# Cross-attention: the transpose of a pair's maxima on VectorE in place of TensorE, and the place of the last two softmax sums

## The reference

```python
x = x + self_attention(layernorm(x), Wq, Wk, Wv, Wo)     # causal, 8 groups of 4 heads of 16
x = x + cross_attention(layernorm(x), ctx, ctx)
x = x + feed_forward(layernorm(x), w_gate, w_up, w_down)

def cross_attention(q, k, v):
    b, d, m = q.shape                      # 4, 512, 512
    qh = q.reshape(b * 8, 64, m); kh = k.reshape(b * 8, 64, -1); vh = v.reshape(b * 8, 64, -1)
    qk = einsum('bdm,bdn->bmn', qh, kh) / sqrt(64)
    sm = softmax(qk, axis=-1)
    return einsum('bmn,bcn->bcm', sm, vh).reshape(b, 512, m)
```

## Time and profile before

| | us |
|---|---|
| Kernel, median of 3 runs (799.4 to 804.82) | 802.62 |
| Profiled execution, its own time | 804.03 |
| Its span, first to last instruction | 801.9 |
| TensorE matmul busy | 769.0 (96%) |
| VectorE busy | 639.2 (80%) |
| ScalarE busy | 491.6 (61%) |
| GpSimd busy | 423.4 (53%) |

### The profile page before, as it was taken

How to read it: one execution, slowest core, us unless ns; L and a number is a source line. 1 busy time by engine, 2 the same in 40 slices (tenths; PEclk the granted TensorE clock), 3 DMA queues, 4 the chain that set the end, 5 groups by cost and what they waited for, 6 DMA issues and landing times.

```text
span 801.9 us, 15448 instructions
## 1 busy us (share of the span) xinstructions
PE 769.0 (96%) x4902; PEld 423.2 (53%) x4902; DVE 639.2 (80%) x1905; ACT 491.6 (61%) x844; POOL 423.4 (53%) x458
## 2 busy tenths in 40 slices
PE   7999999999999999998998999999998899999997
PEld 6777544444444444444875555555543455555543
DVE  7676888889888888971689678888876798888883
ACT  4665467667767767765465455555556565576564
POOL 5554479999999600000334367777785344423321
PEclk9999999999999999999999899999999999999999
DMA  8898665445445212201485534444420011000001
GB/s 290 303 380 290 197 163 138 130 128 142 131 118 148 70 52 64 63 3 53 154 289 193 170 96 130 126 125 120 119 72 11 13 41 40 18 24 27 27 19 47
DMA packets 65760, 94.79 MB, mean 118 GB/s; under 512 B 26928, under 2 KB 38448, under 8 KB 64144
## 3 DMA queue, kind: packets, MB, share of 16 engines
q1 hardware_dynamic: 61216, 80.77, 31.8%
q0 software_dynamic: 3952, 12.98, 6.0%
q10 hardware_dynamic: 512, 0.07, 0.1%
HBM read 72.88 MB, written 20.51 MB: 116 GB/s over the span
## 4 chain that ended last, share of the span: by engine, by line
PE 32%; DVE 11%; issue 4%; ACT 2%; POOL 1%; DMA 1%; SPq 1%; ACTq 0%; DVEq 0%; POOLq 0%
PE r_p L1697 12%; PE r_p L1631 4%; PE r_pn L1644 4%; PE r_p L1727 3%; PE r_pn L1727 3%; DVE r_mx L1408 3%; DVE r_kl L1420 3%; PE r_p L1597 2%; PE r_p L1711 2%; DVE r_stats L1378 1%; DVE r_total L1438 1%; DVE tok L1397 1%; DVE r_inv L1445 1%; PE r_p L1579 1%; DVE r_xl L1391 1%
## 5 line engine op out<-in xcount | busy, mean ns | idle before, releaser
L787 ACT ACTIVATE b_probs<-ab_j 128x512 f32<-128x512 f32 (+1 forms) x352 | 177.1, 560 | 26.7 <-PE ab_j L852 15.8
L148 DVE CUSTOM_DVE_ANT_0 b_junk<-ab_t,mask_qk 128x128 bf16<-128x128 f32 (+2 forms) x243 | 108.8, 486 | 26.9 <-PE ab_t L128 26.8
L852 PE MATMUL ab_j<-qs,ks 98*128 98x512 bf16 (+1 forms) x352 | 123.3, 365 | 1.6 <-DVE a_rest L533 0.8
L1276 ACT ACTIVATE r_probs<-r_p 128x512 f32<-128x512 f32 x128 | 69.5, 599 | 72.3 <-PE r_p L1631 71.0
L148 DVE CUSTOM_DVE_ANT_0 b_junk<-ab_e,mask_qk 128x256 bf16<-128x256 f32 (+2 forms) x237 | 103.7, 482 | 1.8 <-PE ab_e L128 1.5
L1408 DVE TENSOR_REDUCE r_mx<-r_p 128x1 f32<-128x512 f32 x128 | 82.4, 675 | 23.9 <-PE r_p L1597 22.0
L1174 POOL TENSOR_TENSOR r_halves<-r_probs 128x1024 f32<-128x1024 f32 x32 | 77.3, 2414 | 38.5 <-DVE r_total L1438 26.9
L1323 ACT ACTIVATE r_silu<-r_p,r_cg 128x512 f32<-128x512 f32 x64 | 44.3, 692 | 51.4 <-PE r_p L1697 50.2
L870 PE MATMUL ab_pv<-b_probs,v 128*32 128x512 f32 (+3 forms) x1024 | 75.6, 436 | 0.0
L1201 POOL TENSOR_SCALAR r_h<-r_h,r_fh 128x1024 f32<-128x1024 f32 x32 | 37.9, 1198 | 64.1 <-DVE r_fh L1538 64.1
L128 PE MATMUL ab_e<-ks,qs 96*128 96x128 bf16 (+3 forms) x269 | 64.9, 304 | 4.1 <-DVE mx L148 0.9
(11 more groups left out here) (178 smaller groups left out, 1749.9 us busy)
## 6 DMA issues: line engine op xcount, KB each, us to landing
qs<-q_parts SPq DMA_DIRECT2D x32, 192.0 KB, 3.4
q_parts<-a_parts SPq DMA_DIRECT2D x15, 384.0 KB, 6.1
a_wst<-in_w_gate SPq DMA_DIRECT2D x4, 1024.0 KB, 7.5
a_wst<-in_w_up SPq DMA_DIRECT2D x4, 1024.0 KB, 9.9
a_wst<-in_w_down SPq DMA_DIRECT2D x4, 1024.0 KB, 8.4
qs<-q_parts SPq DMA_DIRECT2D x32, 128.0 KB, 3.3
b_wst<-in_w_gate POOLq DMA_DIRECT2D x16, 256.0 KB, 4.0
b_wst<-in_w_up POOLq DMA_DIRECT2D x16, 256.0 KB, 3.1
```

The costliest lines, as they stand in the source:

```text
L148: best = nc.vector.tensor_tensor_reduce(out=junk[:, 2 * (st.use[i, k] % slots) + n, 0:w], in0=bank[:, c:c + w], in1=keep["mask_qk"][:, SEQ ...
L787: nc.scalar.activation(pblock(j % 2, kb)[:, j0:j0 + nj, c:c + w], p2[(NE * j + n) % BANKS2][:, 0:nj * w].rearrange("p (j c) -> p j c", j=n ...
L852: last = nc.tensor.matmul(bank, ks[0:STACK + 2, s, kb * P:(kb + 1) * P], qs[0:STACK + 2, s, j0:j0 + nj, kb * P + c:kb * P + c + w], start= ...
L1276: nc.scalar.activation(probs[:, 2 * (p % 2) + a, blk, :], p2_bank("s", j, n)[:], ACT.Exp, scale=SCALE).then_inc(p2_used, 1)
```

## The change

- The transpose of the maxima moves to VectorE. `mx` grows to 32 columns a pair, of which eight are used, and GpSimd clears it once; the first maximum waits for that. `turn_maxima` on VectorE transposes 128x32 in blocks of 32x32 into `mt`: in partitions 32g to 32g+7 the eight rows of maxima of queries 32g to 32g+31 then stand. TensorE's transpose and its turn in the rotation of `p1` are gone.
- The sign is changed by `unit`, whose rows hold -1.0 and no longer 1.0, so VectorE's negation is gone.
- SyncE sends the rows of a pair in eight DMAs, four partitions of 32 values each, where there were two of four partitions of 128 values.
- Sum 14 stands behind the weighted sums of body 36, and no longer ahead of them. Sum 15 leaves body 38 and stands in feed body 4, behind the third gate and up block on TensorE; its copy on ScalarE (`keep_sums`) moves likewise, behind the third gate.

```diff
-        mx = m.sb("mx", [P, 2, 2 * KD]); mrow = m.sb("mrow", [2 * KD, 2, P], F32R)
+        mx = m.sb("mx", [P, 2, H // 2]); mt = m.sb("mt", [P, 2, H // 2])
...
-            if i >= 2 and i % 2 == 0 and (i - 2) // 2 < PAIRS:
-                p1_use["turn", (i - 2) // 2] = len(p1_use)
...
-        LATE_SUMS = PAIRS - 2
+        LATE_SUMS, LAST_SUM_BODY = PAIRS - 2, E_FIRST + 2
...
             def load_maxima(p):
-                sp.wait_ge(p1_used, p1_use["turn", p] + 1)
+                sp.wait_ge(mt_done, p + 1)
...
                 for a in range(2):
-                    sp.dma_start(mrows[a * H:a * H + 1, p % 2, :].bitcast(F32), mrow[a * KD:(a + 1) * KD, p % 2, :].bitcast(F32)).then_inc(m_in[p % 2], 16)
+                    row = mrows[a * H:a * H + 1, p % 2, :].bitcast(F32).rearrange("o (k g c) -> o k g c", k=KD, g=KD)
+                    for g in range(KD):
+                        at = g * P // KD + KD * a
+                        sp.dma_start(row[:, :, g, :], mt[at:at + KD, p % 2, :]).then_inc(m_in[p % 2], 16)
...
+            nc.gpsimd.memset(mx[:], 0.0)
             nc.gpsimd.memset(unit[:].bitcast(F32), 0.0).then_inc(padded, 1)
             pool.wait_ge(padded, 1)
-            nc.gpsimd.memset(unit[0:1, :].bitcast(F32), 1.0)
-            nc.gpsimd.memset(unit[H:H + 1, :].bitcast(F32), 1.0).then_inc(padded, 1)
+            nc.gpsimd.memset(unit[0:1, :].bitcast(F32), -1.0)
+            nc.gpsimd.memset(unit[H:H + 1, :].bitcast(F32), -1.0).then_inc(padded, 1)
...
                 p = pair_due(i, 8)
-                if p is not None:
-                    act.wait_ge(summed, p + 1)
-                    if due(p):
-                        act.wait_ge(few_in, 32 * p)
-                    nc.scalar.activation(den[:], p2_bank("sum", p)[:], ACT.Copy).then_inc(p2_used, 1)
+                if p is not None and p < PAIRS - 1:
+                    keep_sums(p)
...
                 gate(2)
+                if i == LAST_SUM_BODY:
+                    keep_sums(PAIRS - 1)
                 quantised(i - 1)
...
+                if p1_use["f", i, n] == 0:
+                    dve.wait_ge(padded, 1)
                 dve.wait_ge(p1_full, p1_use["f", i, n] + 1)
...
-            def keep_maxima(p):
-                dve.wait_ge(p1_full, p1_use["turn", p] + 1)
+            def turn_maxima(p):
+                dve.wait_ge(p1_used, STEP * 2 * (p + 1))
                 if p >= 2:
-                    dve.wait_ge(m_in[p % 2], 32 * (p // 2))
-                nc.vector.tensor_scalar(mrow[:, p % 2, :], p1_bank("turn", p)[0:2 * KD, 0:P], -1.0, None, ALU.mult).then_inc(p1_used, 1)
+                    dve.wait_ge(m_in[p % 2], 128 * (p // 2))
+                nc.vector.transpose(mt[:, p % 2, :], mx[:, p % 2, :]).then_inc(mt_done, 1)
...
-            def turn_maxima(p):
-                use = p1_use["turn", p]
-                pe.wait_ge(p1_used, use)
-                nc.tensor.transpose(p1_bank("turn", p)[0:2 * KD, 0:P], mx[:, p % 2, :], keep["ident"][:]).then_inc(p1_full, 1)
...
-                    pe.wait_ge(m_in[p % 2], 32 * (p // 2 + 1))
+                    pe.wait_ge(m_in[p % 2], 128 * (p // 2 + 1))
...
                 p = pair_due(i, 8)
-                if p is not None:
+                if p is not None and p < LATE_SUMS:
                     sum_probs(p)
...
-                p = pair_due(i, 2)
-                if p is not None and p >= 1:
-                    turn_maxima(p)
+                if i == 2 * LATE_SUMS + 8:
+                    sum_probs(LATE_SUMS)
...
                 gate_up(2)
+                if i == LAST_SUM_BODY:
+                    sum_probs(PAIRS - 1)
                 turn_products(j, 1)
```

More of the change, by code:

```diff
@@ L956, in rest_of_layer @@
         scores, p2_used, halved, summed, weighted = (m.sem(s) for s in ("scores", "p2_used", "halved", "summed", "weighted"))
+        mt_done = m.sem("mt_done")
         first_total, second_total = m.sem("first_total"), m.sem("second_total")
@@ L1296, in attend_context, with keep_sums @@
                 p = pair_due(i, 8)
-                if p is not None:
-                    act.wait_ge(summed, p + 1)
-                    if due(p):
-                        act.wait_ge(few_in, 32 * p)
-                    nc.scalar.activation(den[:], p2_bank("sum", p)[:], ACT.Copy).then_inc(p2_used, 1)
+                if p is not None and p < PAIRS - 1:
+                    keep_sums(p)
+            def keep_sums(p):
+                act.wait_ge(summed, p + 1)
+                if due(p):
+                    act.wait_ge(few_in, 32 * p)
+                nc.scalar.activation(den[:], p2_bank("sum", p)[:], ACT.Copy).then_inc(p2_used, 1)
             def quantised(j):
@@ L1428, in early @@
                 if c == TURN_AT:
-                    keep_maxima(0)
+                    turn_maxima(0)
             def attend_context(i):
@@ L1451, in attend_context @@
                 if p is not None and p >= 1:
-                    keep_maxima(p)
+                    turn_maxima(p)
                 p = pair_due(i, 13)
@@ L1607, in early @@
                     first_scores(*BLOCKS_AT[c])
-                if c == TURN_AT:
-                    turn_maxima(0)
             def second_scores(j, b):
```

## The result

The changed kernel takes **823.8 us** (median of 4 runs, 820.89 to 825.22) against 802.62 before: a ratio of 1.0263, with a 95% interval of 1.0218 to 1.0307. It is slower, by some 21 us, where 827 was forecast. The profiled execution has a span of 822.2 us and a time of its own of 823.77.

A forecast was written before the change was run, and what follows sets the result against it. TensorE bounds the kernel before; with eight sends SyncE's queue would, at 11.85 us a pair. 7.2 + 16.9 + 2.8 - 2.8 = +24.1 gives 828.1 by the profiled execution, stated as 827 us, range 807 to 839.

The forecast's parts named there:

- the first loop: SyncE's own queue in a pair: eight sends 5.44, loads 2.15, store's landing 3.06, rden 1.20, together 11.85 us.
- The term of 16.9 us: Pair 4's sends to pair 15's: eleven pairs of 11.85 us, 130.4 against 113.4, so +16.9 us.
- The clock's rival: TensorE's clock falls in the new waits of each pair: +0.75 us for eleven pairs, 838 us; chance 0.14.
- The second loop: From turned maxima through sends, landing and TensorE's wait for the rows to the next transpose: 11.14 us a pair.
- The term of the first four pairs: SyncE's sends of pair 0 to those of pair 4: 45.3 us instead of 38.1, +7.2.
- the landing at the seam: Pair 0's rows, at the start of the pairs, land 7.46 us after its first send.
- The last pair's rows: They land 6.66 us after SyncE's first send, where TensorE needed them after 3.82: +2.8 us.
- The late sums: Moving the last sum in the feed-forward gains 2.5 us and moving sum 14 gains 0.3: -2.8 us.
- The sum: All terms on the profiled execution: 7.2 + 16.9 + 2.8 - 2.8 = +24.1 us, 828.1.
- The cheap-sends rival: Further sends in a row follow on SyncE at 0.36 us and stay hidden: -7.8 us, 795; chance 0.12.
- The block transpose: On VectorE, 128x32 in SBUF in place of the negation, taken at 0.25 us.

The follow-up runs named there:

- run 3: The kernel before, TensorE's transpose and VectorE's negation kept, with the maxima sent in eight pieces of four partitions by 32 values: 852.38 us, ratio 1.0608.
- run 5: The changed kernel, all eight sends, with SyncE's store of the inverse sums moved ahead of the sends: 810.26 us, ratio 1.0112.
- run 4: The changed kernel with the two heads' pieces joined, four sends a pair from eight partitions to two: 792.04 us, ratio 0.9864.
- run 10: The changed kernel with two of the four row groups joined, six sends a pair: 802.66 us, ratio 1.0009.
- run 9: The changed kernel with four joined sends a pair, plus fourteen spare small sends to HBM in SyncE's queue: 817.48 us, ratio 1.0189.
- run 8: The changed kernel with four joined sends a pair and the store of the inverse sums ahead of them: 790.92 us, ratio 0.9873.
- run 7: The changed kernel's eight sends, with the second head's four issued from ScalarE's queue at the head of the odd body: 832.0 us, ratio 1.0403.

## Why the prediction was right

**What bounds, and the first loop.** Borne out. Forecast 11.85 us a pair, measured 12.12 over the eleven. The undisturbed pairs are 11.4 to 11.7, since a send costs 0.65 with its gap in a row of eight and not 0.68 (median issue 573 ns). Three kinds of single longer pair make up the rest: one of 12.75, in which the rden issues took 2.24 us and not 1.15; two of 12.99 and 12.08, whose store took 4.6 and 4.0 us until rden followed; and two of 13.74 and 12.49, in which TensorE's clock fell. In these last two SyncE was idle ahead of the sends, which the prediction had excluded from pair 4 on. The term of 16.9 us measured 19.9 (476.89 to 610.23 is 133.3, against 113.4): six pairs came out shorter than forecast and five longer, and no term of the sum stood for what made them longer.

**The clock's rival** came true in part. Windows of 2 us of the changed kernel:

```profile
540.00:542.00 2.00, 0.55 (x4) 0.18 (x2) 1.42 (x3) 0.27 (x1) 0.53 (x1) 1.00 0.02 5
542.00:544.00 2.00, 0.63 (x4) 0.60 (x6) 0.92 (x2) 0.00 (x0) 1.99 (x1) 0.80 0.90 268
544.00:546.00 2.00, 2.00 (x12) 1.73 (x10) 0.12 (x1) 0.47 (x1) 1.84 (x3) 0.50 0.98 243
```

Behind TensorE's 2.82 us of waiting the clock fell to half. VectorE's keys step took 2.24 us in that pair besides, and the next sends began at 549.60, 13.74 after the last ones, SyncE idle for 2.1 of it. The length of the wait alone does not tell: with waits of 1.3 to 1.6 us the clock stayed, with one of 1.82 (450.89) it fell, and with those of 2.65 and 2.67 (530.55 and 616.64) it stayed. The rival had been priced for every pair, at 0.75 us; the clock fell in two of the eleven and once more in each of the first two. Where it fell in nearly every pair is run 3, and there the time went to 852.

**The second loop** was put at 11.14 us. It measures 10.25 at its shortest (every second pair of run 5, and 6.42 + 3.83 in the changed kernel): landing after the last send's start is 1.8 us, and the keys' low part took 0.9 in place of 1.48. In the other pairs of run 5 it is 11.47, so its mean there, 10.79, is near the forecast. The term of the first four pairs was over-sized: +7.2 was forecast and 4.9 measured (433.88 to 476.89 is 43.0). Half of the 2.3 us between them is the landing at the seam, 6.19 us from the first send to the second scores (433.88 to 440.07) where 7.46 was forecast. The last pair's rows came 6.41 us after the first send (610.23 to 616.64), forecast 6.66: +2.6 for +2.8.

**The late sums.** -2.8 was forecast, and from the last pair's second scores to the end the changed kernel takes 205.6 us against 208.6: -3.0. TensorE doesn't wait at the last sum, as said. Which of the two sums gave more than forecast isn't separated.

**The sum.** 4.9 + 19.9 + 2.6 - 3.0 = 24.4 us from the first send on, forecast 24.1. The spans differ by only 20.3, because the first sends come at 433.88 and not at 437.95. All but some 0.1 us of that is nothing that the change does: from TensorE's last matmul of the projection to the first send it is 2.60 us before (435.35 to 437.95) and 2.50 after (431.38 to 433.88). The profiled execution before had a granted clock of 0.93 and 0.90 in 80 to 120 us and 0.86 in 376 to 400, and the one after 1.00 in all three. The forecast's margin of 3 us over the result is of this size. That the sum itself is only 0.3 us off is luck: the first four pairs were put 2.3 us too high and the eleven behind them 3.0 too low.

**The cheap-sends rival** is refuted for sends of this form (573 ns eight times in a row), with runs 3, 4 and 10 for their number. But the premise behind it, that an issue can be cheap, holds elsewhere: 0.30 us for the same piece to HBM. The Trainium skill ("DMA: Bandwidth & Descriptors", Anatomy of one DMA) gives about 50 ns for the sequencer's dispatch and calls descriptor generation small. That section is on DMAs that GpSimd issues, and these sends are SyncE's, so its figure did not bear on them as the prediction had it; the shortest spare send of run 9 took 0.24 us.

**The block transpose** took 0.21 us, forecast 0.25. What the prediction did not see is how much it is worth once the sends are many: without it (run 3) the second loop runs through TensorE's sum and weighted sum, the clock falls in most pairs, and the kernel takes 852 us.

## What to carry to other kernels

- A DMA queue is an engine: add up its issues and the landings that it waits for in one round of the loop, and compare the sum with the round. It has no busy share, and a small transfer fills it as a large one does. Here joining eight sends of 512 bytes into four of twice the size was worth 32 us (823.8 - 792.0), and turned a loss of 2.6% into a gain of 1.4%.
- Where a queue waits for its own store to land, put the store ahead of other issues. It helps only while the queue is full (run 5, not run 8).
- Before work goes to an idle engine's queue, look at what stands behind it there in that very moment (run 7).

## What the runs showed of the hardware

- The issue time of a small send went with its form and its target: 573 ns from four partitions to one in SBUF, 506 from eight to two in SBUF, 296 from four partitions to HBM (medians). The same store of inverse sums took 0.50 us right behind the vt loads and 0.31 behind the spare sends. Which property sets it stays open.
- The store's landing went with the loads ahead of it in the queue: about 3.2 us right behind vt, 1.3 to 2.0 with five or fourteen small sends between them.
- VectorE's subtraction of 128x512 for the keys' low part takes from 0.68 to 2.24 us in one and the same kernel. What it coincides with was not tried.
- TensorE's granted clock fell to 0.50 behind waits of 1.82, 2.82 and 2.99 us of the changed kernel and stayed at 1.00 behind others of 1.3 to 2.67. In run 3, with waits of about 2 us in nearly every pair, it fell in nine of eleven. What decides between the two was not tried.
